# Key normalisation handed from VectorE to ScalarE and GpSimd, spike offsets from VectorE to ScalarE

## The reference

```
k = (k - mean(k)) / sqrt(var(k) + 1e-5)              # over the 16 features of each of 16 heads
F = retention * F + coef * outer(v_t, k_t)            # per head, 16 x 16, one step per token
y_t = (W_LTM + F) @ q_t
x = x + layernorm(y @ W_o.T)                          # attention half
h = relu(layernorm(x) @ W_fc.T) ** 2 ; y = h @ W_proj.T
mem = 0.9 * mem + y - (mem > 1) ; spikes += (mem_new > 1)   # 5 steps
x = x + layernorm(spikes / 5)                         # feed-forward half
```

## Time and profile before

| | |
|---|---|
| median of 3 runs | 639.84 us (638.0 to 641.08) |
| the profiled execution | 640.17 us, of which the span is 638.4 us |
| PE busy | 498.8 us, 78% |
| DVE busy | 534.7 us, 84% |
| ACT busy | 326.7 us, 51% |
| POOL busy | 384.3 us, 60% |
| granted TensorE clock, mean | 0.887 |

### The profile page before, as it was taken

How to read it: one execution, slowest core, us unless ns; L and a number is a source line. 1 busy time by engine, 2 the same in 40 slices (tenths; PEclk the granted TensorE clock), 3 DMA queues, 4 the chain that set the end, 5 groups by cost and what they waited for, 6 DMA issues and landing times.

```text
span 638.4 us, 7784 instructions
## 1 busy us (share of the span) xinstructions
PE 498.8 (78%) x2272; PEld 326.5 (51%) x2272; DVE 534.7 (84%) x937; ACT 326.7 (51%) x637; POOL 384.3 (60%) x184
## 2 busy tenths in 40 slices
PE   3583478449996999699979997899969995895891
PEld 1341135126673657355745665566636663473670
DVE  4799989997998999899999999999899999821001
ACT  4522123245546754656376646655567355646634
POOL 0026965785567776677677767875687667811101
PEclk9875589679897999989998999798979998988796
DMA  7364476465644575456545664567338634200000
GB/s 236 114 182 134 131 212 183 119 164 146 182 128 122 165 208 139 131 140 189 167 135 156 180 180 119 154 173 209 99 85 230 203 110 132 66 2 0 32 2 33
DMA packets 54729, 87.63 MB, mean 137 GB/s; under 512 B 5408, under 2 KB 19360, under 8 KB 54688
## 3 DMA queue, kind: packets, MB, share of 16 engines
q1 hardware_dynamic: 54112, 87.12, 48.2%
q10 hardware_dynamic: 576, 0.03, 0.1%
HBM read 78.74 MB, written 8.39 MB: 136 GB/s over the span
## 4 chain that ended last, share of the span: by engine, by line
PE 53%; issue 16%; POOL 10%; ACT 10%; DVE 10%; DMA 1%; POOLq 0%; ACTq 0%; DVEq 0%
PE p_c L346 13%; PE p_c L371 12%; PE p_a L281 7%; POOL prod L875 6%; PE p_y L324 6%; DVE state L733 5%; PE p_c L337 4%; ACT sign L547 3%; PE p_c L354 2%; PE p_a L301 2%; POOL x1t L891 2%; PE p_y L319 2%; DVE p_u L723 2%; ACT oo L468 1%; PE p_c L363 1%
## 5 line engine op out<-in xcount | busy, mean ns | idle before, releaser
L875 POOL TENSOR_TENSOR prod<-state,qf 128x1024 f32<-128x1024 f32 x128 | 302.8, 2371 | 147.5 <-DVE state L733 126.1
L733 DVE TENSOR_TENSOR_SCAN state<-ret,p_u 128x512 f32<-128x512 f32 x256 | 308.8, 1207 | 0.0
L723 DVE TENSOR_TENSOR p_u<-vrep,p_k 128x512 f32<-128x512 f32 x256 | 171.1, 674 | 2.5 <-ACT p_k L479 2.5
L346 PE MATMUL p_c<-wproj_sb,ht 128*128 128x256 f32 x512 | 116.1, 382 | 1.3 <-ACT ht L537 1.3
L371 PE MATMUL p_c<-x1t,wfc_s 128*128 128x512 f32 x384 | 99.4, 411 | 11.7 <-POOL x1t L891 10.6
L346 PEld LDWEIGHTS p_c<-wproj_sb,ht 128*128 128x128 f32 x512 | 95.7, 190 | 24.3 <-issue 9.2
L281 PE MATMUL p_a<-xt,wqkv_s 128*128 128x512 f32 x276 | 82.4, 437 | 13.9 <-POOL xt L891 5.4
L371 PEld LDWEIGHTS p_c<-x1t,wfc_s 128*128 128x128 f32 x384 | 74.4, 197 | 32.9 <-POOL x1t L891 13.7
L324 PE MATMUL p_y<-prod,summer 128*32 128x512 f32 x512 | 75.1, 661 | 8.5 <-POOL prod L875 8.5
L281 PEld LDWEIGHTS p_a<-xt,wqkv_s 128*128 128x128 f32 x276 | 53.1, 202 | 47.8 <-issue 16.3
L535 ACT ACTIVATE hr<-p_c 128x512 f32<-128x512 f32 x64 | 38.2, 597 | 36.8 <-PE p_c L371 34.9
(11 more groups left out here) (106 smaller groups left out, 481.0 us busy)
## 6 DMA issues: line engine op xcount, KB each, us to landing
vrep<-v_rows SPq DMA_DIRECT2D x256, 256.0 KB, 3.6
xa<-in_x SPq DMA_DIRECT2D x8, 512.0 KB, 5.4
v_rows<-vf SPq DMA_DIRECT2D x16, 256.0 KB, 2.0
x<-in_x SPq DMA_DIRECT2D x8, 512.0 KB, 4.7
out<-x SPq DMA_DIRECT2D x8, 512.0 KB, 3.4
ht<-in_w_fc SPq DMA_DIRECT2D x1, 1024.0 KB, 7.4
wproj_sb<-in_w_proj SPq DMA_DIRECT2D x1, 1024.0 KB, 9.9
state<-in_w_qkv SPq DMA_DIRECT2D x1, 512.0 KB, 5.5
```

Of the source, the lines that this page charges most:

```text
L346: last = pe.matmul(p_c[(u + 1) % 2][:, 0:D], ht[:, f, tokens(u)], wproj_sb[:, f, :], start=(f == 0), stop=(f == FT - 1))
L723: v.tensor_tensor(p_u[n % NU][:, :], vrep[:, n % NV, :], p_k[:, :], ALU.mult).then_inc(S["hebb_done"], 1)
L733: v.tensor_tensor_scan(state[:, s % NS, i, :], ret[:, r:r + 1].broadcast_to([P, L]), p_u[n % NU][:, :], 0.0, ALU.mult, ALU.add).then_inc(S ...
L875: p.tensor_tensor(prod[:, s % NZ, :, :], state[:, s % NS, :, :], qf[:, s // HS, :].unsqueeze(1).broadcast_to([P, 2, L]), ALU.mult).then_in ...
```

## The change

Three things change, in the same places of the schedule.

- `norm_k` moves from VectorE to GpSimd. As GpSimd can't read PSUM, ScalarE first copies the transposed scale from `p_a` to a new SBUF tile `ks` (`move_scale`, in slots 6 and 15). GpSimd multiplies `ks` and `kc` in slot 7, behind read 6, and in slot 15, behind read 14. The first of the 16 products stays on VectorE in the prologue.
- TensorE frees `p_a` by the semaphore of the copy (`k_moved`) and no longer by that of the product (`k_done`).
- The four offsets of the spike norm (L687, VectorE, 128x1 each) become ScalarE instructions in slot 12: one that negates `rdev` into `nrd` (128x4), and four that multiply a mean by a column of `nrd`. ScalarE waits for its own result twice, ahead of the four and ahead of the norm.

```diff
@@ TensorE
             def turn_x(b, t):
-                pe.wait_ge(S["k_done"], at(2 * b))
+                pe.wait_ge(S["k_moved"], at(2 * b - 1))
             def project_v(b, half):
                 pe.wait_ge(S["xt_low"], at(KT * (b + 1)))
-                pe.wait_ge(S["k_done"], at(2 * b + half))
+                pe.wait_ge(S["k_done"], 1)
+                pe.wait_ge(S["k_moved"], at(2 * b + half - 1))
@@ ScalarE
+            def offsets4(b):
+                act.wait_ge(S["n4_step"], at(b + 1))
+                nc.scalar.activation(nrd[:, :], rdev[3][:, :], ACT.Identity, scale=-1.0).then_inc(S["n4_turned"], 1)
+                act.wait_ge(S["n4_turned"], at(b + 1))
+                for u in range(TILES):
+                    last = nc.scalar.activation(nmr[:, u:u + 1], moments[3][:, u, 0:1], ACT.Identity,
+                                                scale=nrd[:, u:u + 1])
+                last.then_inc(S["n4_offset"], 1)
             def norm4(b):
-                act.wait_ge(S["n4_step"], at(2 * (b + 1)))
+                act.wait_ge(S["n4_offset"], at(b + 1))
+            def move_scale(b, half):
+                act.wait_ge(S["k_done"], at(2 * b + half))
+                copy(p_a[:, :], ks[:, :], "k_scale", 2 * b + half + 1, "k_moved")
                     if s == 6:
+                        if now: move_scale(g, 1)
                         if after: copy_xt(b, 0)
                     if s == 12:
                         if after: key_deviation(b, 0)
-                        if two_before: norm4(b2)
+                        if two_before:
+                            offsets4(b2)
+                            norm4(b2)
-                    if before and s == 15: hidden(b1, 5)
+                    if s == 15:
+                        if after: move_scale(b, 0)
+                        if before: hidden(b1, 5)
@@ VectorE
-            def spike_offsets(b):
-                dve.wait_ge(S["n4_step"], at(2 * b + 1))
-                for u in range(TILES):
-                    last = v.tensor_scalar(nmr[:, u:u + 1], moments[3][:, u, 0:1], rdev[3][:, u:u + 1], -1.0, ALU.mult,
-                                           ALU.mult)
-                last.then_inc(S["n4_step"], 1)
-            def norm_k(b, half):
-                dve.wait_ge(S["k_scale"], at(2 * b + half + 1))
-                dve.wait_ge(S["k_bank"], at(2 * b + half))
-                v.tensor_tensor(kf[:, :], p_a[:, :], kc[:, :], ALU.mult).then_inc(S["k_done"], 1)
-                    if now and s == 6: norm_k(g, 1)
-                    if two_before and s == 12:
-                        scales(4, b2)
-                        spike_offsets(b2)
+                    if two_before and s == 12: scales(4, b2)
-                    if after and s == 15: norm_k(b, 0)
@@ GpSimd
+            def norm_k(b, half):
+                pool.wait_ge(S["k_moved"], 2 * b + half)
+                pool.wait_ge(S["k_bank"], at(2 * b + half))
+                p.tensor_tensor(kf[:, :], ks[:, :], kc[:, :], ALU.mult).then_inc(S["k_done"], 1)
                     if s > 0 and now: read(g, s - 1)
+                    if now and s == 7: norm_k(g, 1)
                     if before and s == 6: add_attention(b1)
                     if two_before and s == 13: add_feed_forward(b2)
+                    if after and s == 15: norm_k(b, 0)
```

More of the change, by code:

```diff
@@ L113, in build @@
         nmr = sb("nmr", [P, TILES])
+        nrd = sb("nrd", [P, TILES])
         xa = sb("xa", [P, TILES, D])
@@ L123, in build @@
         kf = sb("kf", [P, L])
+        ks = sb("ks", [P, L])
         qf = sb("qf", [P, HALVES, L])
@@ L158, in build @@
             n1_stats n1_var n1_dev n1_step n1_done  xt_turned xt_done xt_high xt_low
-            k_proj k_sq k_var k_dev k_rdev k_spread k_scale k_done k_bank  v_proj v_done  q_proj q_done
+            k_proj k_sq k_var k_dev k_rdev k_spread k_scale k_moved k_done k_bank  v_proj v_done  q_proj q_done
             v_out hebb_done state_done prod_done sum_done y_done
@@ L163, in build @@
             up_done relu_done h_done down_done yf_done
-            sign_done count_done spk_done n4_stats n4_var n4_dev n4_step n4_done res_done""".split()}
+            sign_done count_done spk_done n4_stats n4_var n4_dev n4_step n4_turned n4_offset n4_done res_done""".split()}
         v_in = [sem(f"v_in{i}") for i in range(NV)]
@@ L673, in statistics @@
                 dve.wait_ge(S[f"n{n}_stats"], at(b + 1))
-                dve.wait_ge(S[f"n{n}_step"], at(b if n < 4 else 2 * b))
+                dve.wait_ge(S[f"n{n}_step"], at(b))
                 for u in range(TILES):
@@ L832, in _ @@
             key_reciprocal(0, 0)
-            norm_k(0, 0)
+            dve.wait_ge(S["k_scale"], 1)
+            v.tensor_tensor(kf[:, :], p_a[:, :], kc[:, :], ALU.mult).then_inc(S["k_done"], 1)
             def iteration(g, now, before, two_before, after):
```

## The result

The changed kernel takes 658.42 us in the median of four runs (654.23 to 660.21), the one before 640.46 us beside it (638.0 to 642.86): a ratio of 1.0271, 95% interval 1.0236 to 1.0305. The profiled execution took 658.28 us, of which the span is 656.5 us. The forecast was 650 us with a range up to 657: the direction was right, the size was forecast too small by 8 us, and the measured time lies outside the range.

What follows compares the result with a forecast made beforehand. The prediction took the chain of TensorE and ScalarE to bound the steady part. Its terms 0.6 + 1.8 + 2.9 + 3.4 + 1.6 = 10.3 us on 640.17 us gave 650 us, range 641 to 657.

Steps and rivals of the forecast that it cites:

- Place 1: Slots 12 to 15: late norm and GpSimd product delay the last read and slot 1's sums; 0.9 us reach the chain.
- Place 2: Slots 5 to 8: GpSimd's product in slot 7 delays the key bank's copy to p_k; chain 1.4 us late.
- g = 4 and 5, L337 fast: 2 x 1.4: Iterations 4 and 5, attention output (L337) at the higher clock level: 1.4 us late in each, +2.9 us.
- g = 1: Iteration 1, no spike norm yet: only the slot 7 product delays VectorE's start on the key bank, +0.6 us.
- g = 0: Iteration 0: GpSimd late by under 1 us with the wide weights, caught up at the next iteration's start; counted 0.
- g = 2: Iteration 2: no delay handed over from the iteration before; 0.
- g = 7: Iteration 7, the last with scans, bound by VectorE: key products late behind GpSimd's reads, +3.4 us in all.
- tail: Iterations 8 and 9: the spike norm comes later because of its offsets on ScalarE, +1.1 and +0.5 us.
- The clock makes it worse: Rival: TensorE's added waits before L337 and the count cost it the higher clock level; 655 us, chance 0.19.
- VectorE was the bound: Rival: the key bank arrives in time and VectorE's 12.4 us come out; 628 us, chance 0.08.
- No change: Rival: the delays shrink below what TensorE's own waits absorb, only the end is longer; about 640.5 us, chance 0.12.
- The two engines block each other: Rival: each GpSimd product holds VectorE up for its whole length, 19 us on top; 669 us, chance 0.03.

Runs made afterwards that it cites:

- e9: Changed kernel plus five unused TensorE products an iteration ahead of the key variance of slot 2; 652.33 us, ratio 1.0161 to the kernel before.
- e1: Kernel before with only the spike norm's offsets moved to ScalarE, the key product staying on VectorE; 644.49 us, ratio 1.0057.
- e2: Kernel before with only the scale's move and the key product on GpSimd, the offsets staying on VectorE; 648.83 us, ratio 1.0092.
- e11: Changed kernel plus unused TensorE products in all the idle places filled in e10; 644.86 us, ratio 1.0030 to the kernel before.
- e7: Kernel before plus five unused TensorE products an iteration ahead of the key variance of slot 2; 637.30 us, ratio 0.9942.
- e8: Kernel before plus one extra unused 128x1024 GpSimd product between reads 14 and 15 of iterations 1 to 6; 649.36 us, ratio 1.0149.
- e4: Changed kernel with the key product back on VectorE, reading the scale's SBUF copy; 654.58 us, ratio 1.0200 to the kernel before.
- e6: Changed kernel plus unused TensorE products: four ahead of slot 1's last sums, five ahead of slot 2's key variance; 654.36 us, ratio 1.0207.
- e12: Kernel before with only the spike norm's offsets moved to ScalarE, plus all the filling products of e10; 631.12 us, ratio 0.9839.
- e10: Kernel before plus unused TensorE products ahead of the key variance, the second spike count and, near the end, further waits; 628.09 us, ratio 0.9796.

## Why the prediction was right about the direction and wrong about the size

**What held.** The bound of the steady part was the chain of TensorE and ScalarE; 13.1 us less work on VectorE gained nothing. Place 1 came out nearly as worked out: norm 1.1 us later, product 1.25 to 1.28 us, wait of the sums 1.00 us, VectorE idle 2.3 us at slot 0 (about 3 had been forecast). Place 2 as well, in e9. e1 and e2 show the arithmetic of place 1: with either delay by itself the sums do not wait, with both they do.

**The step that failed** is "g = 4 and 5, L337 fast: 2 x 1.4", the assumption under it that an attention output which was fast would stay fast. The delay itself was right: 65.3 + 1.4 = 66.7 us, and e9 has 66.9. But in the changed kernel those two periods are 68.0, 2.7 us over before, as TensorE's clock fell to the lower level in each of them. The same term is missing elsewhere. By stage, from the profiled executions:

| stage | forecast | measured | why |
|---|---|---|---|
| up to the first p_k copy | 0 | +1.0 | prologue, ahead of the change |
| to slot 8 of g = 1 | +0.6 | +1.2 | 4.1 late at slot 8 of g = 0, 2.9 won back in g = 1 |
| g = 2 | 0 | +1.3 | mean clock 0.83, before 0.90 |
| g = 3 and 6 | +1.8 | +1.9 | slow before and after |
| g = 4 and 5 | +2.9 | +5.5 | level lost in both |
| g = 7 | +3.4 | +4.1 | |
| tail | +1.6 | +3.05 | mean clock 0.84, before 0.88 |

The measured column adds up to 18.1 us. Of the 7.8 us beyond the forecast, 2.6 are the level in g = 4 and 5, 1.3 lie in g = 2 and 1.4 in the tail, both at a lower mean clock than before; together 5.3. 1.0 is the prologue, and 1.5 the terms of g = 1, 3, 6 and 7. The term of g = 0 ("late by under 1 us", and counted as 0) was wrong too: slot 8 of g = 0 comes 4.1 us late, as it does in e9 and e11. For g = 2 the clock is borne out by e7 and e9, both with the attention output at the higher level: the stage takes 66.4 and 66.5 us there, so the delays alone add 0.1. For the tail the clock is a reading and not a proof. The rows of the two stages are, first before and then after,

```profile
128.77:196.86 68.09, 57.54 (x268) 39.83 (x272) 62.50 (x96) 33.03 (x67) 44.64 (x22) 0.90 0.55 147
...
524.79:638.40 113.61, 78.16 (x337) 55.43 (x336) 39.61 (x91) 60.70 (x115) 35.66 (x17) 0.88 0.12 37
```

```profile
131.01:200.44 69.43, 60.24 (x268) 41.53 (x272) 60.59 (x92) 34.41 (x67) 47.62 (x24) 0.83 0.55 144
...
539.84:656.50 116.66, 79.90 (x321) 57.08 (x323) 37.04 (x77) 63.58 (x129) 35.25 (x17) 0.84 0.13 36
```

In the tail TensorE waits 2.21 us for the ReLU behind the small group, 1.15 before, and the up-projection after it takes 5.99 us, not 4.38 (TensorE, after):

```profile
618.03 5.99 PE L374 MATMUL p_c<-x1t,wfc_s 128*128 128x512 f32 x18 [2.21 <-ACT hr L551]
```

With five filling products an iteration, which take the level out of it, the changed kernel stands at 1.0161 of before. That is what the forecast comes to, 650.5 / 640.17 = 1.016. That agreement is luck, as errors cancel in it: e9's outputs are all at the higher level, and before had three at the lower. Against e7, with both at the higher level, the delays alone cost 15.2 us net and not 10.3: 3.7 up to slot 8 of g = 1 (0.6 forecast), 0.1 in g = 2, 6.3 in g = 3 to 6 (4.7 forecast), 4.1 in g = 7 (3.4) and 1.0 in the tail (1.6).

**The rivals.** "The clock makes it worse" is what happened, with the mechanism given: longer waits ahead of the attention output, two fast periods made slow, 655 us. It had a chance of 0.19. The argument against it, that nothing in the trace says how much idleness is too much, was no argument against it: the trace showed the same idle stretch with and without the fall. By the timeline the wait is 1.44 us both times: the one from 367.60 on had the clock at 1.00 after it, as shown above, and the one from 432.90 on a fall some 2 us after its end. The rows of the second, before:

```profile
432.90:434.30 1.40, 0.00 (x0) 1.00 1.01 307
...
436.20:437.20 1.00, 1.00 (x5) 0.67 1.13 361
```

The level already fell in three of six attention outputs, and with one more us of idleness ahead of them it fell in five (the changed kernel) and six (e8). "VectorE was the bound" falls with the result itself, 13.1 us less work and a span 18.1 us longer, and, for this order of the work, with e11. "No change" is nearest in e1, with the offsets alone: 0.6% slower. "The two engines block each other" holds for two operands in SBUF (e4) and had been excluded rightly for this change.

**Open.** Why the clock stays up in one iteration of the changed kernel with the same waits (attention output of 514.31, 3.70 us) is not explained. A product behind read 13 or behind read 15 was not tried.

## What to carry to other kernels

Add up the delays that a change puts on one queue before you compare them with the reserve at its end: two harmless parts can overrun it together. Where a stretch of TensorE is fast in some iterations and slow in others, count a change that adds idle time ahead of it at the slow duration in all of them, and try the reverse too: cheap products in TensorE's idle time were worth 2% here, and moving work between the other engines was worth nothing. Work taken off the busiest engine is worth nothing while another chain sets the period, and when that engine has hardly any idle time left it matters when its inputs arrive (e11).

## What the runs showed of the hardware

- TensorE's level fell inside the attention output after two idle stretches of 1.0 and 1.2 us, in five of six iterations, though the engine was busy between and behind them. With 1.25 us of small products in the stretch ahead of the key variance it fell in none of the 36 attention outputs of iterations 2 to 7 in the six kernels so filled (e6, e7, e9 to e12). In iteration 8 the attention output took 5.2 to 5.8 us in e6, e7 and e9, which have no filling right ahead of it, and 3.69 in e10 to e12, which have.
- Before, the second spike count takes 2.32 us after 4.85 us of waiting (at 401.34); with most of the wait filled it takes 1.25 us (TensorE, e10):

```profile
392.61 3.19 PE L378 MATMUL p_c<-ident_b 128*128 128x512 bf16 x14 [0.19 <-ACT yf L490]
397.28 1.25 PE L354 MATMUL p_c<-sign,ident_b 128*128 128x512 bf16 x5 [1.47 <-ACT sign L558]
```

- A 128x512 product on VectorE with both operands in SBUF took 1.94 us in the mean beside a busy GpSimd (e4), against 0.67 us with one in PSUM, and stretched GpSimd's block by 0.44 us.
